# Second mixture stage: normed rows scattered to per-expert DRAM slots instead of gathered tile by tile

## The reference, cut to what matters

```
u      = layernorm(X)
shared = (a * gelu(g)) @ Ws2,            a, g = split(u @ Ws1)
logits = (u @ Wr + br) / 1.5             12 experts, the best two of each token are kept
y_e(u) = (a * gelu(g)) @ We2[e] + be2[e],   a, g = split(u @ We1[e] + be1[e])
X      = X + 0.5 * (shared + sum over the two chosen experts of softmax weight * y_e(u))
```

## Time and profile before

| what | us |
|---|---|
| runs of the kernel before, median (lowest to highest) | 1375.27 (1372.22 to 1377.22) |
| the profiled execution, its own time | 1371.62 |
| its span in the trace | 1369.7 |
| PE busy | 1169.8 (85%) |
| DVE busy | 926.9 (68%) |
| ACT busy | 844.7 (62%) |
| POOL busy | 793.0 (58%) |
| mean granted share of the TensorE clock | 0.953 |

### The profile page before, as it was taken

How to read it: one execution, slowest core, us unless ns; L and a number is a source line. 1 busy time by engine, 2 the same in 40 slices (tenths; PEclk the granted TensorE clock), 3 DMA queues, 4 the chain that set the end, 5 groups by cost and what they waited for, 6 DMA issues and landing times.

```text
span 1369.7 us, 36413 instructions
## 1 busy us (share of the span) xinstructions
PE 1169.8 (85%) x12703; PEld 875.4 (64%) x12704; DVE 926.9 (68%) x2479; ACT 844.7 (62%) x2476; POOL 793.0 (58%) x708
## 2 busy tenths in 40 slices
PE   5899898998979999799989899898778857768884
PEld 2667675666745555457768567685677736457773
DVE  7998669986856776689867888788432376643233
ACT  3999768998434555489985899944243524314343
POOL 6788358874654352288844878543666532266653
PEclk9999999999989999999999999998799979879997
DMA  7011100111000000000110001132455520135564
GB/s 221 17 25 25 28 15 16 25 25 28 17 2 3 3 3 3 2 9 22 32 29 9 19 21 25 28 86 66 116 158 178 168 71 0 44 109 161 176 178 119
DMA packets 69808, 78.21 MB, mean 57 GB/s; under 512 B 25094, under 2 KB 50501, under 8 KB 69509
## 3 DMA queue, kind: packets, MB, share of 16 engines
q1 hardware_dynamic: 64133, 64.70, 16.9%
q0 software_dynamic: 5504, 11.28, 2.9%
HBM read 54.60 MB, written 8.78 MB: 46 GB/s over the span
## 4 chain that ended last, share of the span: by engine, by line
PE 61%; DVE 12%; ACT 10%; DMA 6%; issue 4%; POOL 1%; SPq 1%; POOLq 1%; another core or an unknown queue 1%; ACTq 0%; DVEq 0%
PE bank L1849 10%; ACT pB L795 5%; PE bank L916 5%; DMA arena<-arena 4%; PE bank L1863 4%; PE bank L637 3%; PE bank L559 3%; PE bank L600 3%; PE bank L928 3%; PE bank L1515 3%; PE bank L1536 3%; PE bank L545 3%; PE bank L551 2%; PE bank L612 2%; PE bank L1547 2%
## 5 line engine op out<-in xcount | busy, mean ns | idle before, releaser
L2109 DVE SCALAR_TENSOR_TENSOR act_b<-bank,vec,gl 128x128 f32<-128x128 f32 x258 | 75.1, 345 | 183.7 <-ACT gl L1933 76.2
L864 POOL TENSOR_TENSOR rn<-ss,mhalf 128x16 f32<-128x16 f32 x64 | 187.2, 2925 | 6.9
L1933 ACT ACTIVATE gl<-bank,vec 128x128 f32<-128x128 f32 x258 | 76.0, 365 | 126.3 <-PE bank L1849 109.3
L1849 PE MATMUL bank<-arena 128*128 128x128 f32 x1032 | 141.1, 290 | 3.1 <-DVE act_b L2109 1.7
L1849 PEld LDWEIGHTS bank<-arena 128*128 128x128 f32 x1032 | 131.4, 204 | 10.2 <-issue 7.2
L2186 POOL DMA_INDIRECT arena<-u_rows,inv_u x86 | 84.8, 986 | 71.7 <-remote 34.6
L795 ACT ACTIVATE pA<-bank,nb,rn 128x128 f32<-128x128 f32 x256 | 113.5, 484 | 3.1 <-DVE nb L726 3.1
L795 ACT ACTIVATE pB<-bank,nb,rn 128x128 f32<-128x128 f32 x256 | 113.3, 478 | 1.7 <-DVE nb L726 1.7
L2192 POOL DMA_INDIRECT y_rows<-stg,inv_u x86 | 85.4, 993 | 41.4 <-issue 20.7
L850 POOL TENSOR_TENSOR arena<-arena 128x512 f32<-128x512 f32 x64 | 81.6, 1275 | 47.6 <-DVE nb L726 36.9
L857 POOL TENSOR_TENSOR arena<-arena 128x512 f32<-128x512 f32 x64 | 81.3, 1271 | 43.0 <-DVE arena L689 16.3
(11 more groups left out here) (335 smaller groups left out, 3131.5 us busy)
## 6 DMA issues: line engine op xcount, KB each, us to landing
arena<-in_L_ffn_We SPq DMA_DIRECT2D x86, 384.0 KB
arena<-arena SPq DMA_DIRECT2D x64, 128.0 KB, 2.3
arena<-in_L_ffn_We SPq DMA_DIRECT2D x3, 768.0 KB, 7.5
arena<-U SPq DMA_DIRECT2D x32, 64.0 KB
u_rows<-U SPq DMA_DIRECT2D x2, 1024.0 KB, 5.8
U<-y_rows SPq DMA_DIRECT2D x8, 256.0 KB, 4.2
uT<-y_rows SPq DMA_DIRECT2D x8, 256.0 KB, 4.9
arena<-U SPq DMA_DIRECT2D x32, 63.5 KB
```

Of the source, the lines that this page charges most:

```text
L864: pool.tensor_tensor(rn[:, q % 4, :, :], ss[:, 1, :].rearrange("p (a h) -> p a h", a=2), mhalf[:, :].rearrange("p (a h) -> p a h", a=2), A ...
L1849: m = pe.matmul(bank[q % 2][:, j * P:(j + 1) * P], we1[q][:, half * HR + j * P:half * HR + (j + 1) * P], xT[:, q, :], start=True, stop=True)
```

## The change

Only mixture 2 (`k0 == 1`) and the LA phase ahead of it change in what they do. In this order:

- `x_slots`, a DRAM tensor of 224 blocks of 64 KB, gives each expert 16 blocks. Between sites 0 and 1 SP writes zeros to all of it in seven DMAs (`blank_slots`).
- In LA the logits of a chunk come one step earlier, and for chunks 0 to 2 DVE picks the experts (`chunk_picks`), PE counts (`chunk_counts`) and DVE adds a running count and gets the slot of each (token, expert) pair (`chunk_slots`), inside the pipeline.
- POOL scatters the tiles of U by these slots, two indirect DMAs a tile (`row_out`), 32 in all: four ahead of the last `power` of LA, 20 after POOL's own drain at the end of LA, and eight in the mixture, with the `te` step after the first two of these.
- Chunk 3 is picked and counted at the start of the mixture, and the tables of tiles come from the running counts. All 32 one-hots are built by DVE. The ring is still multiplied, now for the scatter's list alone. The softmax and the turn of the router's weights come later.
- The 43 gathers of mixture 2 and its store of U are gone. SP loads each tile's 64 KB block with a plain DMA (`x_rows_in`), which reads the expert's number and that expert's first block out of SBUF: four blocks after the first four We1 loads, and then block n+1 ahead of the weights of tile n. The first waits for all 32 scatters.
- POOL issues only scatters in the loop.

```diff
+        def blank_slots(sp):
+            w = SLOT_BLOCKS // N_BLANK
+            for n in range(N_BLANK):
+                sp.dma_start(x_slots[n * w:(n + 1) * w, :, :].rearrange("b p d -> p b d"),
+                             bc(blank[:, :].unsqueeze(1), [P, w, D])).then_inc(s.stored, 16)
...
             def x_turn(i, o, q):
                 n, buf = 8 * i + 4 * o + q, 4 * o + q
-                pe.wait_ge(LD_X[buf], 16 * (x_loads(k0, buf) + i + 1))
+                if k0:
+                    pe.wait_ge(GAT[q], 16 * (2 + 2 * i + o + 1))
+                else:
+                    pe.wait_ge(LD_X[buf], 16 * (x_loads(k0, buf) + i + 1))
...
+            if k0:
+                chunk_counts(pe, NCH - 1)
             up(0, 0)
...
+            if k0:
+                chunk_picks(dve, NCH - 1, taken[0])
+                dve.wait_ge(s.r_self, taken[0] + 4)
+                dve.tensor_tensor(rw[:, :, 0], top[:, :, 1], top[:, :, 0], ALU.subtract).then_inc(s.r_m12, 1)
+                chunk_slots(dve, NCH - 1, taken[0] + 4)
+                taken[0] += 7
+                tables()
...
-                if m % 8 in OH_POOL:
+                if m % 8 in OH_POOL and not k0:
                     continue
...
+            if k0:
+                for t in range(NT - CT, NT):
+                    for k in range(2):
+                        row_out(pool, t, k, r_base(1) + 7)
+                    if t == NT - CT:
+                        names()
+                power()
+                pool.wait_ge(s.r_self, r_base(k0) + R_SCATTER[k0])
+                for n in range(NU):
+                    scatter(n)
+                return
...
+            def x_rows_in(n):
+                e = expert(sp, n)
+                first = sp.value_load(sbase_u[0:1, bass.ds(e, 1)], min_val=0, max_val=(E - 1) * SLOT_E)
+                if not n:
+                    for q in range(4):
+                        sp.wait_ge(ST_Y[q], 16 * (quarter(q) + ROWS_OUT))
+                if n >= 4:
+                    sp.wait_ge(s.x_ps, base + n - 3)
+                sp.dma_start(xg[:, n % XG, :], x_slots[bass.ds(first + n, 1), :, :].rearrange("o p d -> p (o d)"))\
+                    .then_inc(GAT[n % 4], 16)
...
             for n in range(NU):
                 if n >= WB:
                     sp.wait_ge(s.x_up, 2 * (base + n - WB + 1))
+                    if k0:
+                        for m in ([n, n + 1] if n == WB else [n + 1] if n + 1 < NU else []):
+                            x_rows_in(m)
                 e = expert(sp, n)
                 sp.dma_start(we1[n % WB], a["L1_ffn_We1"][bass.ds(e, 1), :, :].rearrange("o k n -> k (o n)"))\
                     .then_inc((s.ld_e0, s.ld_e1, s.ld_e2, s.ld_e3)[n % WB], 16)
+                if k0 and n == WB - 1:
+                    for m in range(WB):
+                        x_rows_in(m)
...
+        def chunk_picks(dve, c, event):
...
+            dve.wait_ge(s.r_lg, c + 2)
+            dve.scalar_tensor_tensor(lg[:, ts, :], LA_LG.rearrange("p (t e) -> p t e", e=E)[:, ts, :], 1.0 / TAU,
+                                     bc(br_row[:, :].unsqueeze(1), [P, CT, E]), ALU.mult, ALU.add)\
+                .then_inc(s.r_read, 1)
...
+            for t in range(ts.start, ts.stop):
+                m = dve.max(top[:, t, :], lg[:, t, :])
+            after(m)
+            for t in range(ts.start, ts.stop):
+                m = dve.max_index(idx[:, t, :], top[:, t, :], lg[:, t, :])
+            after(m)
...
             for c in range(NCH):
                 if c + 1 < NCH:
                     v_bias(c + 1)
+                if c == NCH - 1:
+                    pool.wait_ge(s.stored, 16 * (N_BLANK + 1))
+                    for t in range(CT):
+                        row_out(pool, t, t % 2, LA_EVENT(0) + 7)
                 power(c, 1)
-            phase_end(pool, "pool", ph)
+            pool.drain().then_inc(s.ph_pool, 1)
+            for t in range(CT):
+                row_out(pool, t, 1 - t % 2, LA_EVENT(0) + 7)
+            for c in (1, 2):
+                for t in range(c * CT, (c + 1) * CT):
+                    for k in range(2):
+                        row_out(pool, t, k, LA_EVENT(c) + 7)
```

More of the change, by code:

```diff
@@ L1749, in build, with sh_up @@
         RING_INV = B[0][:, 256:256 + NXT]
-        def sh_up(g):
-            return B[1 + 2 * g], B[2 + 2 * g]
+        def sh_up(k0, g):
+            return B[6 if k0 and not g else 1 + 2 * g], B[2 + 2 * g]
         XIN, XY, SH_OUT = B[0], (B[6], B[7]), B[5]
@@ L1886, in mx_pe @@
             up(1, 0)
-            counts()
+            if not k0:
+                counts()
             up(1, 1)
@@ L1890, in mx_pe @@
             up(2, 1)
-            weights_turn()
+            if not k0:
+                weights_turn()
             up(3, 0)
@@ L1992, in prefix @@
                 return src
[L1995 to L2025, removed]
@@ new lines, in chunk_slots, with after @@
+        def chunk_slots(dve, c, event):
+            ts = slice(c * CT, (c + 1) * CT)
+            steps = itertools.count(event + 1)
+            def after(m):
+                m.then_inc(s.r_self, 1)
+                dve.wait_ge(s.r_self, next(steps))
+            dve.wait_ge(s.r_cum, c + 2)
+            dve.tensor_tensor(place[:, ts, :], LA_CUM[:, 0:CT * E].rearrange("p (t e) -> p t e", e=E),
+                              bc(run[:, :].unsqueeze(1), [P, CT, E]), ALU.add)
+            after(dve.tensor_tensor(sbase[:, :], LA_CUM[:, CT * E:(CT + 1) * E], run[:, :], ALU.add))
+            for k in range(2):
+                m = dve.tensor_tensor(rank2[:, k, :, :], oh[k][:, ts, :], place[:, ts, :], ALU.mult)
+            m.then_inc(s.r_read, 1)
+            dve.wait_ge(s.r_read, 2 * c + 2)
+            dve.tensor_copy(run[:, :], sbase[:, :])
+            after(dve.tensor_reduce(slotf[:, :, :].rearrange("p k t -> p (k t)"),
+                                    rank2[:, :, :, :].rearrange("p k t e -> p (k t) e"), AX_X, ALU.add))
+            after(dve.tensor_copy(slot_u[:, :, ts], slotf[:, :, :]))
@@ L2367, in la_pe @@
             v_proj(0)
-            for i in range(-1, NCH + 3):
+            for i in range(-1, NCH + 2):
                 if has(i - 1):
                     out_proj(i - 1)
+                if has(i - 3) and i - 3 < NCH - 1:
+                    chunk_counts(pe, i - 3)
                 if has(i - 2):
```

270 lines of the change are left out of this document (206 added, 64 removed).

## The result

| | kernel before | changed kernel |
|---|---|---|
| median of four runs | 1375.32 us (1372.22 to 1377.22) | 1388.88 us (1386.26 to 1390.84) |
| profiled execution | 1371.62, span 1369.7 | 1386.26, span 1384.2 |

The ratio is 1.0117, with a 95% interval of 1.0094 to 1.0141: slower. The spans of the two profiled executions lie 14.5 us apart. The forecast was 1380 in a range of 1355 to 1393, with slower as the likeliest direction.

The account below looks back on a forecast made before the run. Bounds named: POOL's drain ending LA, routing to the first gather, and a loop slowed by dense indirect DMAs. Terms summed to +5.2 us (1371.6 to 1376.8 profiled; 1380.5 against the median, given as 1380), range 1355 to 1393.

Parts of the forecast that it names:

- likeliest case: The forecast's own case: SP's loop pitch 2.8 to 3.0 us, a change of +1 to +9 us, chance 0.50.
- The loop: Mixture 2's tiles: SP's issue work becomes the bound at 2.9 us a tile; last result on ACT at 1350.8 instead of 1344.4.
- The blanks: Zero writes between the sites: 14.7 MB, at most some 81 us, hidden while SP and the DMA engines idle; cost 0.
- Rival A: Tiles 5 to 42: PE, not SP, sets the loop, 81 us instead of 110, result 1353; chance 0.15.
- LA: Attention ahead of mixture 2: DVE's added picks and slot steps delay its end by 4.5 us, bounds 0 and +9.
- POOL's last `power` moreover stands behind four scatters: End of LA: four scatters of 1.28 us wait for slot step 0, so `power` ends at 1177.2 instead of 1172.72.
- POOL's drain still holds everybody: End of LA: the drain, 7.1 us again, ends at 1184.4; the other engines end at about 1183.7, just inside it.
- POOL to the first row: After POOL's drain: 28 scatters of 1.28 us plus `te` reach 1221.4, last landing 1223.6; DVE's routing hides under them.
- SP ahead of the loop: SP's first four weight loads before block 0: 1 us added, bounds 0 and +6; block 0 asked for at 1224.6.
- Rival C: After LA's drain: 28 scatters without pause slow SP's loads and the ring's completions; +12 us, 1387; chance 0.19.
- dense indirect DMAs on POOL slow the others' signals, and the gathers are what makes them dense: Old mixture 2 loop: 3.13 us a tile while gathers are issued, 1.91 after the last one.
- What is behind it (loading back, adding, POOL's drain) is unchanged: After the loop's last scatter: the kernel's tail takes the same time as before.

Follow-up runs that it names:

- e10: Changed kernel with the four rows-out ahead of POOL's last `power` in the attention issued behind the drain instead; one run, 1361.38 us.
- c_after: The changed kernel with no edit, run as a control on another chip than the first comparison: 1357.81 us, ratio to the kernel before 1.0248.
- c_before: The kernel before with no edit, run for its profile on another chip than the first comparison: 1323.63 us in one run.
- e5: Changed kernel scattering only each row's copy for its first expert, 12 rows-out behind the drain instead of 28 (half the right rows left out): 1337.23 us.
- e8: Changed kernel with DVE's block table, no POOL drain ending the attention, SP waiting for the table itself: 1326.43 us, ratio to the kernel before 1.003.

## Why the prediction was right or wrong

The forecast named the right direction and the time lies in its range, but above its likeliest case (1375 to 1385), and the change was +14.5 us where +5.2 was summed. That it held owes something to the chip, and so to luck: on the other chip where the changed kernel ran as it is, the change costs 34.5 us, and the range reached to +18.

**The loop.** Right, and it was the term said to decide. SP's pitch was put at 2.9 us from three register reads and two issues and measured at 2.92 (2.91 on another chip); one read was put at 0.56 and measured at 0.52. The stretch from weights 4 to weights 42 came out at 109.1 us against 110.2. The Trainium skill's rule, DMA: Bandwidth & Descriptors, section Issuing engines are not separate DMA queues, that the issuing sequencer's time is "usually small relative to the DMA itself", was no guide here: SP's work on two loads a tile was the bound, and taking two of three reads away gave 26 us. Rival A needed a pitch below 2.76 and fell. Its price was a little too good besides: PE needs 2.22 us a tile over the whole loop, where rows without shared products and tail showed 1.91 to 2.12.

**The blanks.** Right: cost 0.

**LA.** The size was right, the reason in part. From chunk 1's power on POOL to chunk 3's it took 14.0 us before and 19.05 after (1160.47 to 1179.52), and on the other chip 14.0 and 19.0: the picks and slot steps cost 5.0 us on both, where I took 4.5. But the step "POOL's last `power` moreover stands behind four scatters" is wrong: e10 shows that the power waits for DVE's moments whatever POOL does before, so the whole 5.0 is DVE's. The other 3.1 us of the 8.1 had arisen before chunk 1's power, 0.9 of it ahead of the attention. In c_after against c_before that same first part was 2.6 us shorter (1134.29 beside 1136.86), so it is spread between executions: one step of it on POOL, from the values' bias of one chunk to that of the next, takes 6.6 us in some executions and 8.3 in others, with either kernel (6.6 in before and c_after, 8.3 in after and c_before).

**The barrier.** The step "POOL's drain still holds everybody" was wrong. The drain ended 7.4 us behind the power, not 7.1 (at 1188.3, not 1184.4), but the others' work, put at 1183.7, ended later still: for counts, picks and slots of chunk 2 PE and DVE wait for one another (2.4 us on DVE at 1187.95), and DVE begins mixture 2 at 1191.64. That cost nothing, since only POOL's rows-out count.

**POOL to the first row.** Right: 28 rows-out, 1.27 us apart, with all tables hidden behind them; they only ended 4.4 us later than forecast, since the drain ended 3.9 us later. Experiment e5 confirms that tile 0 waits for them.

**SP ahead of the loop.** Of the terms that belong to the change ahead of the loop, this one was mis-sized most. I added 1 us to the undisturbed loads, with +6 as the bound. Block 0 came 7.1 us later than forecast, of which 4.4 are the later rows-out and 2.7 this term: from the end of the last row-out's issue to block 0 it took 5.9 us, where the forecast had 3.2. In c_after it took 2.35. (The 3.2 had a slip in it: the 2.24 us to the landing count in the earlier trace rows from the start of the issue, and were added to its end.) Rival C's mechanism (28 indirect DMAs in a row slow SP and DVE) did occur on the first chip: DVE's one-hots took 23.2 us (1206.7 to 1229.9) instead of the 9.6 that I gave them, and SP's second load 7.7 us. But on the other chips the same burst slows nobody (one-hots 9.1 us, SP's loads 1.10 to 1.47 apart), and there the change costs more, not less. So C has some 3 us of the 14.5 on the first chip and nothing on the other; it is not why the change is slower.

**What was taken for the kernel's and was the chip's.** The step "dense indirect DMAs on POOL slow the others' signals, and the gathers are what makes them dense" read the first profile rightly and was no law of the kernel. The forecast of +5 us rested on a loop before that lost about 0.7 us a tile in this way. On the one other chip where it was profiled it lost none of it, and the loop of mixture 1, which is the same in all kernels, ran 18.5 to 18.9 us shorter in every profile on the three others than in that of the kernel before on the first. On the other chip that was profiled the old loop is held by POOL's own issue, 2.57 us for a gather and a scatter, still below SP's 2.92, and the change is 2.5% slower. Why the first chip behaves otherwise stays open.

**The sum.** Forecast +5.2, measured +14.5 between the profiled spans. The missing 9.3 us by steps: last power 3.6, drain 0.3, from there to block 0 3.2, first tile and weights 4 1.3, the loop -1.1, and 2.5 from the last weights to the last result, which took 8.4 us instead of 5.9 (4.2 from the load's issue to PE's product instead of 3.0, 4.1 from there to the result instead of 2.9); the tail, forecast 1.2 us shorter than before, was 1.7 shorter. Its step "What is behind it (loading back, adding, POOL's drain) is unchanged" was wrong for the drain: 7.16 us instead of 8.51. So the sizes that failed are SP ahead of the loop (2.7), the last tile (2.5), the stretch from block 0 to weights 4 (1.3) and, less, the attention and the rows-out (0.5 each); 3.1 us are spread.

## What to carry to other kernels

Count the sequencer's instructions per tile on the queue that gets a new load: a dynamic address costs a register read of half a microsecond each on SP, and three reads with two issues outweighed 2.2 us of matrix products. Prepare the address as one number on an engine that has time, and derive the rest by a shift. When a transfer is moved ahead of a loop in bulk, the loop's first tile pays the whole bulk (here 28 x 1.27 us), while the gathers that it replaces ran beside the products. And before a slow loop is blamed on a neighbour's DMAs, look at the same kernel on a second chip.

## What was not expected of the hardware

- The same kernel took 1375 us on one chip and 1321 to 1323 on three others, and of the 48.0 us between the two profiles of the kernel before 18.8 and 21.5 lie in the two loops with a gather and a scatter a tile: in mixture 2 3.16 us a tile against 2.46, with granted clocks of 0.94 and 1.00 there and "remote" waits on the first only.
- A drain of POOL took 5.00 to 9.83 us wherever POOL had issued indirect DMAs since the drain before, longer the more of them there were (43 to 161), and the same on every chip. It could be replaced by a wait on POOL's own last operation, but then the next drain took 2.5 to 2.7 us more.
- Going without the drain, POOL ran ahead of DVE, and the 7 us won came back as a wait of 6.73 us at the next table. In e8, with the names behind 22 rows-out again and SP's wait moved to the table itself, they stayed won.
